# Streamed transformer: the feed-forward rows' moments behind the addition of chunk 1, their root behind the rotation of q

## What is computed

```
def _layer(x, wqkv, qs, ksc, wo, lg, lb, w1, b1, w2, b2):
    h = shift_token(x)
    q, k, v = jnp.split(h @ wqkv, 3, axis=-1)      # then 8 heads of 64
    q, k = l2norm(q) * qs, l2norm(k) * ksc
    q, k = rotary_xpos(q, k)
    x = x + local_attention(q, k, v) @ wo          # window 64, looks one window back
    h = shift_token(x)
    mu, var = h.mean(-1, keepdims=True), h.var(-1, keepdims=True)
    h = (h - mu) / jnp.sqrt(var + 1e-05) * lg + lb
    a, g = jnp.split(h @ w1 + b1, 2, axis=-1)
    return x + (a * gelu(g)) @ w2 + b2
```

## Time and profile before

| | |
|---|---|
| median of the runs | 6142.15 us |
| profiled execution | 6135.76 us, its span 6134.0 us |
| granted TensorE clock, mean | 0.972 |
| TensorE matmul busy | 5688.0 us, 93% |
| VectorE busy | 4321.5 us, 70% |
| ScalarE busy | 3850.9 us, 63% |
| GpSimd busy | 2914.1 us, 48% |

### The profile page before, as it was taken

The page is one execution under the profiler, slowest core; times in us unless marked ns, Lnnn a source line. Parts: engine busy times, 40 slices in busy tenths (PEclk is TensorE's granted clock), DMA queues, the critical chain, the costliest instruction groups (busy, mean ns, idle before and its releaser), DMA issues. The chain is left out here.

```text
span 6134.0 us, 102245 instructions
## 1 busy us (share of the span) xinstructions
PE 5688.0 (93%) x33833; PEld 3013.5 (49%) x33833; DVE 4321.5 (70%) x9755; ACT 3850.9 (63%) x8213; POOL 2914.1 (48%) x2774
## 2 busy tenths in 40 slices
PE   8999999689997999999999979999999999987868
PEld 3444444422222566666666634444444444455558
DVE  4555555178885777777888768888888888867655
ACT  2444444256665677777777757777777777755436
POOL 1224326456776766666666533323323323324458
PEclk9999999799998999999999989999999999999879
DMA  2001001221110111111111110000000000013123
GB/s 47 15 15 39 26 15 45 75 58 40 32 35 30 42 30 34 32 32 39 40 46 46 34 35 11 13 19 11 13 19 11 13 19 11 11 43 116 45 95 97
DMA packets 304270, 219.34 MB, mean 36 GB/s; under 512 B 27890, under 2 KB 279668, under 8 KB 303492
## 3 DMA queue, kind: packets, MB, share of 16 engines
q1 hardware_dynamic: 284578, 177.38, 11.2%
q0 software_dynamic: 12544, 29.71, 1.4%
q10 hardware_dynamic: 6626, 5.72, 0.3%
HBM read 97.11 MB, written 73.87 MB: 28 GB/s over the span
## 5 line engine op out<-in xcount | busy, mean ns | idle before, releaser
L3864 PE MATMUL a_scores_ps<-a_kT,a_q_mixed 128*128 128x512 f32 x2048 | 1046.4, 593 | 3.2 <-ACT a_probs L3674 3.1
L3874 PE MATMUL a_acc_ps<-a_probsT,a_v_post 128*128 128x512 f32 x2048 | 1042.8, 592 | 0.4 <-DVE a_probsT L3767 0.4
L3674 ACT ACTIVATE a_probs<-a_scores_ps,a_neg_max 128x512 f32<-128x512 f32 x1024 | 703.0, 687 | 428.6 <-DVE a_neg_max L3757 419.3
L3757 DVE TENSOR_REDUCE a_neg_max<-a_scores_ps 128x1 f32<-128x512 f32 x1024 | 693.4, 677 | 202.0 <-PE a_scores_ps L3864 196.9
L3767 DVE STREAM_TRANSPOSE a_probsT<-a_probs 128x512 f32<-128x512 f32 x1024 | 715.5, 699 | 135.9 <-PE a_acc_ps L3874 112.5
L3679 ACT ACTIVATE a_probs<-a_probs,a_inv_sum 128x512 f32<-128x512 f32 x1024 | 727.7, 711 | 0.8 <-DVE a_inv_sum L3762 0.8
L3045 DVE TENSOR_REDUCE a_neg_max<-a_pair_ps 128x2 f32<-128x1024 f32 (+3 forms) x512 | 417.7, 824 | 354.5 <-PE a_pair_ps L3141 349.4
L2850 ACT ACTIVATE a_probsT<-a_pair_ps 128x1024 f32<-128x1024 f32 (+3 forms) x512 | 359.4, 704 | 484.4 <-PE a_pair_ps L3154 482.9
L3874 PEld LDWEIGHTS a_acc_ps<-a_probsT,a_v_post 128*128 128x128 f32 x2048 | 389.0, 190 | 490.9 <-issue 488.8
L3864 PEld LDWEIGHTS a_scores_ps<-a_kT,a_q_mixed 128*128 128x128 f32 x2048 | 384.4, 190 | 476.0 <-issue 438.2
L3620 POOL TENSOR_TENSOR a_q_mixed<-a_qT,a_pre 128x512 f32<-128x512 f32 x248 | 250.1, 1040 | 759.7 <-PE a_scores_ps L3864 759.7
(11 more groups left out here) (420 smaller groups left out, 11863.5 us busy)
## 6 DMA issues: line engine op xcount, KB each, us to landing
f_v_even<-f_v_odd SPq DMA_DIRECT2D x224, 130.0 KB, 2.3
a_v<-a_v_rows SPq DMA_DIRECT2D x256, 64.0 KB, 2.1
f_x_tiles<-routed_x SPq DMA_DIRECT2D x72, 193.0 KB
attention_out<-a_s_out SPq DMA_DIRECT2D x48, 256.0 KB, 2.3
routes_y_rows<-a_zeros SPq DMA_DIRECT2D x32, 256.0 KB, 2.8
a_parts<-routes_y_rows SPq DMA_DIRECT2D x32, 256.0 KB, 3.4
f_x<-x_after SPq DMA_DIRECT2D x32, 256.0 KB
f_gx<-x_after SPq DMA_DIRECT2D x32, 256.0 KB, 3.1
```

The lines of the kernel that those rows point to most:

```text
L3674: act.activation(probs[:, n % NPR, :], scores_ps[n % NS][:], ACT.Exp, bias=neg_max[:, n % NS:n % NS + 1], scale=1.0, accum_out=row_sum[:, ...
L3757: dve.tensor_reduce(neg_max[:, n % NS:n % NS + 1], scores_ps[n % NS][:], AX.X, ALU.max, negate=True).then_inc(max_ready, 1)
L3864: pe.matmul(scores_ps[n % NS][:], q_mixed[:, g % 2, i].rearrange("f a q -> f (a q)"), kT[:, par, :], start=True, stop=True).then_inc(score ...
L3874: pe.matmul(acc_ps[par][:], v_post[:, g, i, :], probsT[:, g % NT, i, :], start=(p == 0), stop=(p == U - 1)).then_inc(products_done, 1)
```

## The change

Two calls move, and nothing else. On GpSimd, `layer_root` is issued behind `rotate_q` in chunk 1, no longer between `rotate_k` and `rotate_q`. On VectorE, `moments_of_rows` is no longer issued in chunk 0 between the two halves of `unit_max`, ahead of the first half of `keep_o`, but in chunk 1, behind `add_out` and ahead of `rotate_parts` of k.

```
@@ GpSimd's body
                     if exists(n + o1):
                         rotate_k(j.plus(o1), n + o1, c1)
+                    if exists(n + o1):
+                        rotate_q(j.plus(o1), n + o1, c1)
                     if c == 1 and exists(n - 2):
                         layer_root(j.plus(-2))
-                    if exists(n + o1):
-                        rotate_q(j.plus(o1), n + o1, c1)
                     if exists(n):
                         add_k_parts(j, c)
@@ VectorE's body
                     if exists(n + o5):
                         add_out(j.plus(o5), n + o5, c5)
+                    if c == 1 and exists(n - 2):
+                        moments_of_rows(f)
                     if exists(n):
                         rotate_parts(j, n, c, K)
...
                     if exists(n + o2):
                         unit_max(j.plus(o2), n + o2, c2, 1)
-                    if c == 0 and exists(n - 2):
-                        moments_of_rows(f)
                     if c == 1 and n >= 0 and exists(n + 1) and layer_of(n + 1) == 0:
                         rows.moments_of(dve, chain, j.plus(1).number())
```

## The result

| | before | changed |
|---|---|---|
| median, 12 runs each | 6143.73 us | 6159.75 us |
| profiled execution | 6135.76 us, span 6134.0 | 6158.86 us, span 6157.2 |

What follows compares the result with a forecast made beforehand. TensorE was taken to bound the stage, stalling 1.23 us per item for VectorE's addition. Shifted to v's projection, the stall makes each of 30 items 0.25 us longer, 7.5 us in all: 6149.6 us, range 6133 to 6158.

Steps and rivals of the forecast that it cites:

- What bounds the stage: Layer 1's streamed transformer: TensorE sets the pace, with one stall of 1.23 us per item for VectorE's addition in chunk 1.
- Step 1: VectorE ahead of the addition: keep_o at 30.20, maxima 30.74, product 31.46; 0.68 us becomes a wait for TensorE.
- Step 2: GpSimd's rotate_q leads VectorE's product by 0.05 us and holds it; the addition's stall falls from 1.23 to 0.10 us.
- rival A: VectorE's product precedes rotate_q, 0.81 us gained per item: 6136 in 13 items (chance 0.10), 6118 in all (0.06).
- Step 3: VectorE's k parts finish at 35.57 instead of 35.29; TensorE's v projection waits 1.28 us, starting at 35.63.
- Step 4: TensorE's v projection, now waited for, is charged 0.10 us; the mask starts at 36.59 instead of 36.34.
- Step 5: GpSimd's later root is free by 0.2 us before add_k_parts, normalise_rows by 1.8; TensorE's turning of hn costs nothing.
- The sum: Over the stage's 30 items, each longer by 0.25 us: 7.5 us, giving 6149.6 us, 0.12% slower.
- B: TensorE's stall just goes, with no wait for k's parts replacing it: 37 us gained, 6105, chance 0.04.
- C: GpSimd's rotate_q is stretched in its new slot, 1.71 us instead of 1.26: 21 us slower, 6163, chance 0.14.
- the prediction's rule: On the port VectorE and GpSimd share, whichever starts first holds it for the whole instruction; the product loses behind rotate_q.

Runs made afterwards that it cites:

- experiment 6: Kernel before with only the root moved behind rotate_q, plus add_bias waiting in chunk 0 for VectorE's first product with the norms; ratio 0.9932, 6087.6 us.
- experiment 3: Kernel before with only VectorE's moments moved behind the addition, the root still ahead of rotate_q; ratio 0.9964.
- experiment 2: Kernel before with only GpSimd's root moved behind rotate_q, the moments staying in chunk 0; ratio 0.9948, 6097.83 against 6129.84 us.
- 5: Changed kernel with the moments one place further down, behind rotate_parts of k; ratio to the kernel before 0.9992.
- the first of 4: Kernel before, nothing moved, with rotate_q in chunk 1 waiting for VectorE's second product with the norms of chunk 0; ratio 0.9952.
- the second of 4: Changed kernel with rotate_q in chunk 1 waiting for VectorE's second product with the norms of chunk 0; ratio to the kernel before 0.9969.

## Why the prediction was right, point by point

*What bounds the stage.* Right. One stall per item, at the place where VectorE's gapless stretch meets TensorE; experiment 6, which removes it, leaves no other of that size in the steady items.

*Step 1.* Forecast were `keep_o` at 30.20, maxima at 30.74 and the product at 31.46, that is 2.45, 2.99 and 3.71 us behind the maxima of the item; measured 2.46, 3.02 and 3.73. VectorE's wait for the product of TensorE was 0.61 us (0.68 forecast).

*Step 2.* The decisive one, with a lead of 0.05 us for `rotate_q` in the 13 last items and 0.16 in the others. It led by 0.07 and 0.19, and the product was held in 29 of 30 items. The chain was reckoned from starts and ends of rows that, but for two items, repeat within 0.02 us from item to item in each half of the stage, which is why so thin a margin could be trusted. TensorE's wait for the addition was 0.21 us in the 13 last items, where 0.10 was forecast; q's projection still started at 5.20, as forecast. The thirtieth item shows rival A. In it `rotate_k` starts 0.28 us later than in its neighbours, as it did in the kernel before (2.83 us behind the maxima at 2456.22); the prediction counted that item among the 17 with 2.54, and they are 16. GpSimd, then VectorE's second product and addition:

```profile
2475.35 1.04 POOL L834 TENSOR_TENSOR f_turned_rows<-f_cos_part,f_k_norms 128x512 f32<-128x512 f32 x1
2476.35 1.27 POOL L841 TENSOR_TENSOR f_turned_rows<-f_cos_part,f_sin_part 128x512 f32<-128x512 f32 x1
...
2476.26 0.16 DVE L1065 TENSOR_TENSOR f_neg_max<-f_row_max,f_q_norms 128x4 f32<-128x4 f32 x1
2476.34 0.29 DVE L1082 TENSOR_TENSOR f_xk<-f_xk,f_q_ps 128x128 f32<-128x128 f32 x1
```

The product, at 3.73 us behind the maxima, came 0.13 us before `rotate_k`'s end and 0.09 us before `rotate_q`'s start. It took 0.16 us, so it went in between the two, although `rotate_q` followed at once; v's projection started at 6.84, and the item was 47.17 us long instead of 48.10. Rival A's price was put at 0.81 us below the kernel before; here it was 0.96 below this item of before (48.13) and 0.67 below an ordinary one (47.84). For the 13 last items, for which it was reckoned, the price was right: with the product free, in experiments 3 and 4, their period is 46.70 against 47.50.

*Step 3.* Addition forecast at 4.87, measured 4.88; L1047 forecast at 6.48, measured 6.48; v's projection forecast at 7.88, measured 7.89. The forecast wait of 1.28 us was counted from the start that TensorE could have had, 0.44 us behind that of the group ahead; counted so it was 1.28 (3006.40 - 3005.12). The profile counts from the end of that group and shows 1.12.

*Step 4.* v's projection took 1.12 us instead of 1.02 and its follower started 0.96 behind it: the charge of 0.10 us was right. The row that it was taken from doesn't support it. q's projection behind the products of L1282 takes 1.12 us whether TensorE waited for it or not, here in chunk 3 of the kernel before, and in chunk 1 of experiment 6, both without a wait:

```profile
3069.97 1.12 PE L1230 MATMUL f_q_ps<-f_w_qkv,f_hT 128*128 128x512 f32 x2
```

```profile
3005.43 1.13 PE L1232 MATMUL f_q_ps<-f_w_qkv,f_hT 128*128 128x512 f32 x2
```

What the prediction took for the cost of a wait was there the difference between two projections that stand behind different groups. That v's cost the same 0.10 us more was luck. For v it is measured: 1.02 us where it isn't waited for (before, experiments 2, 5, 6 and the first of 4), 1.12 where it is (changed, experiment 3 and the second of 4). The item is longer by 0.26 (48.10 against 47.84, 47.76 against 47.50); 0.25 was forecast.

*Step 5.* The root ended at 3006.18, and `add_k_parts` started at 3006.42, with a wait of 0.24 us for k's parts, as reckoned. TensorE turned `hn` 0.26 us later than before, without a wait of its own.

*The sum.* 6.8 us in the stage, forecast 7.5; 0.11% against 0.12%. Of the 30 items 28 are longer by 0.23 to 0.28 us, the one above is shorter by 0.96, and one (maxima at 2807.38) is longer by 0.60: in it VectorE stood idle for 0.26 us ahead of k's parts, for nothing that the profile shows. The comparison over 12 runs gave 0.21%. What the sum left out is that stretches outside the changed stage vary by more than the effect: 14 us between two traces of one kernel. The range reached to 6158 us for other reasons, so that it covers the first comparison (6155.0) is luck; the mechanism accounts for 6.8 of the 13 us. A forecast that names "the same" up to 0.2% and sits at 0.12% needs that variation in its chances: 0.14 for slower was too little.

*The rivals.* B (the stall just goes) is excluded by the new line of waits; C (`rotate_q` stretched) by its 1.27 us. A came true in one item.

*What the prediction didn't see* was its own best use. It named the product that is held and who holds it, but took the change as given and didn't ask what each half alone would do to the meeting. The same rows say it: with the moments in chunk 0 the product comes at 4.90 behind the maxima, and a `rotate_q` right behind `rotate_k` is over at 4.92.

## What to carry to other kernels

Where VectorE and GpSimd run side by side, look for VectorE rows far longer than their shape, and for the GpSimd row that ends with them; the cost of an order is then decided by which of two instructions starts first, and a move on one engine must be laid over the timeline of the other. If a short instruction on the critical path is held by a long one that isn't, let the long one wait for the short one: a wait on the engine with slack gained 0.5% here with nothing moved. And when an instruction passes others on an engine that has no gap, follow the stretch to its last customer: the stall only moves along it.

## What the runs showed of the hardware

Not every GpSimd instruction holds VectorE's product. The root's kind, `pow` with a small tile, didn't in any row of these traces. In the changed kernel, GpSimd's norms of k and VectorE's product in chunk 1:

```profile
3009.94 1.67 POOL L827 TENSOR_TENSOR f_k_norms<-f_kept_sums,f_neg_half 128x8 f32<-128x8 f32 x1
...
3011.24 0.16 DVE L1065 TENSOR_TENSOR f_neg_max<-f_row_max,f_q_norms 128x4 f32<-128x4 f32 x1
```

The product started 1.30 us into a `pow` that lasted 1.67, and took 0.16 us. In experiment 2 the second product likewise took only 0.20 us although the root ran from 3014.30 on. So the prediction's rule needs a limit: that a GpSimd instruction which started first is waited out was seen for those that read tiles of 128x512. Over the whole stage of the kernel before, 128 of the 256 products with the norms began while such a row was open (L834, L841, L854), and every one of them ended 0.01 to 0.03 us behind its end; the 47 that began during a `pow` took 0.16 to 0.20 us.

A wait that TensorE has to make can cost more than its length: v's projection took 1.12 us instead of 1.02 where it had been waited for, and what followed started 0.96 us behind it instead of 0.86. It isn't so everywhere: q's took 1.12 us with a wait of 1.23 us and 1.13 without any.
